# Last stage of a one-core transformer block: turning tiles by transposing transfers instead of on TensorE, and a new order of the engines' work

## What is computed

```python
h = layernorm(x) * (1 + ca) + sa
x = x + ga * attention(h)                  # 16 heads; the 409 queries of largest norm in each head
h = layernorm(x) * (1 + cb) + sb
gate = fp4_linear(h, w_gate); y = fp4_linear(h, w_up)      # 1408 columns each
x = x + gb * fp4_linear(silu(gate) * y, w_down)
# fp4_linear quantises both operands in blocks of 16: scale = max|block| / 6, values rounded to a grid of eight magnitudes
```

## Time and profile before

| | |
|---|---|
| median of 3 runs | 3645.56 us (3643.36 to 3648.74) |
| the profiled execution's own time | 3647.05 us |
| its span | 3645.2 us |
| TensorE's granted clock over the span | 0.957 of full speed |
| TensorE busy (matmul) | 3308.7 us, 91% |
| VectorE, GpSimd, ScalarE busy | 2764.1, 1512.2, 1035.5 us (76%, 41%, 28%) |
| DMA | 252.71 MB, mean 69 GB/s |

### The profile page before, as it was taken

How to read it: one execution, slowest core, us unless ns; L and a number is a source line. 1 busy time by engine, 2 the same in 40 slices (tenths; PEclk the granted TensorE clock), 3 DMA queues, 4 the chain that set the end, 5 groups by cost and what they waited for, 6 DMA issues and landing times. The chain is left out here.

```text
span 3645.2 us, 50953 instructions
## 1 busy us (share of the span) xinstructions
PE 3308.7 (91%) x16784; PEld 1498.4 (41%) x16784; DVE 2764.1 (76%) x3797; ACT 1035.5 (28%) x1454; POOL 1512.2 (41%) x1311
## 2 busy tenths in 40 slices
PE   5999997036999999999986999999999999999998
PEld 2554553021323332333323555555555555555554
DVE  4677675975666666666645898989898989898986
ACT  1332331003555555555541111111111111111111
POOL 0332331004555555555533444444444444445442
PEclk8999998567999999999997999999999999999999
DMA  5656556102222222222212100010101010101000
...
DMA packets 194398, 252.71 MB, mean 69 GB/s; under 512 B 58581, under 2 KB 114261, under 8 KB 193493
## 3 DMA queue, kind: packets, MB, share of 16 engines
...
## 5 line engine op out<-in xcount | busy, mean ns | idle before, releaser
L1038 DVE TENSOR_REDUCE top<-ps_max 128x1 f32<-128x1024 f32 (+1 forms) x512 | 618.5, 1219 | 340.9 <-PE ps_max L1171 340.8
L1117 ACT ACTIVATE p<-ps_exp,p_bias 128x820 f32<-128x820 f32 x512 | 483.0, 943 | 457.6 <-PE ps_exp L1197 457.6
L1208 PE MATMUL ps_out<-p,v_tok 128*33 128x410 f32 x2048 | 453.0, 521 | 0.0
L1007 POOL DMA_INDIRECT o_d<-o_rows,chosen x256 | 249.0, 973 | 446.6 <-DVE o_rows L1064 373.7
L1642 ACT ACTIVATE silu<-f_g 128x512 f32<-128x512 f32 (+1 forms) x192 | 107.8, 561 | 801.5 <-PE f_u L1711 801.5
L1171 PE MATMUL ps_max<-k_max,q_max 96*128 96x512 f16 (+1 forms) x1024 | 314.4, 389 | 1.1 <-DVE top L1038 0.8
L1197 PE MATMUL ps_exp<-q_exp,k_exp 98*128 98x410 f16 x1024 | 266.7, 342 | 44.7 <-ACT p L1117 44.7
L1711 PE MATMUL f_g<-gu,xT_lo 128*128 128x512 f16 (+1 forms) x768 | 278.3, 362 | 0.0
L1709 PE MATMUL f_g<-gu,xT_hi 128*128 128x512 f16 (+1 forms) x768 | 278.1, 362 | 0.0
L1710 PE MATMUL f_g<-gu,xT_hi 128*128 128x512 f16 (+1 forms) x768 | 278.1, 362 | 0.0
L1709 PE MATMUL f_u<-gu,xT_hi 128*128 128x512 f16 (+1 forms) x768 | 277.5, 361 | 0.0
(11 more groups left out here) (201 smaller groups left out, 6417.7 us busy)
## 6 DMA issues: line engine op xcount, KB each, us to landing
...
a_in<-o_d SPq DMA_DIRECT2D x64, 256.0 KB, 2.6
```

What stands on the lines that cost most here:

```text
L1007: pool.indirect_dma_start(o_rows, bass.IndirectOffsetOnAxis(ap=con["chosen"][0:n, t, h:h + 1], axis=0), o_rows_of[u][0:n, t, :], None).the ...
L1038: ve.tensor_reduce(top[0:rows_of(t), t, half:half + 1], ps_max[c % 2][0:rows_of(t), :, :].rearrange("p a n -> p (a n)"), AX.X, ALU.max, ne ...
L1117: act.activation(p32[k % PB][:, :, :], ps_exp[:, :, 0:NQ], ACT.Exp, bias=con["p_bias"][:, 0:1], scale=scale).then_inc(p_done, 1)
L1208: last = pe.matmul(ps_out[at:at + VCOLS, 0:NQ], v_tok[u][:, t, :], p32[k % PB][:, s, :], start=k == 0, stop=k == STEPS - 1)
```

## The change

All three turns (attention's rows, quantised `xq`, quantised hidden tile) leave TensorE. Each tile is split into high and low fp16 parts first, in SBUF and in its own layout: ScalarE reads `a_in`, `xq1` or `xq2` (`high_of_a`, `high_of_x`, `high_of_hidden`; the hidden tile in one instruction of 1408 columns), VectorE the same and the high part (`low_of_a`, `low_of_x`, `low_of_hidden`). Then SP issues two transposing transfers, of the high and of the low part (`turn_a`, `turn_x`, `turn_hidden`). The two PSUM banks that held turned tiles become third banks for gate and up. The second normalisation moves from VectorE to ScalarE (`normalise`, an Identity activation with scale 1/deviation and a shift, which GpSimd now works out as a third small step in `deviation`). `take_attention` multiplies by `ga` while it takes the product out; GpSimd adds `ga * bo`, worked out once, to `x` instead (`residual`). The front of a tile (attention's product, residual, moments, normalisation, modulation) is done two slots ahead of its gate and up instead of one, and the order in each engine's slot is new. The result of the down product is added and stored two slots behind the tile instead of three. A few semaphores are shared between stages, and seven slots are written out at the end instead of three.

```diff
-        ps_t = [m.ps(f"f_t{k}", [P, 512]) for k in range(2)]
-        ps_g = [m.ps(f"f_g{k}", [P, 512]) for k in range(2)]
-        ps_u = [m.ps(f"f_u{k}", [P, 512]) for k in range(2)]
+        ps_g = [m.ps(f"f_g{k}", [P, 512]) for k in range(3)]
+        ps_u = [m.ps(f"f_u{k}", [P, 512]) for k in range(3)]
...
+def turn_a(t):
+    if has(t, -1):
+        hold(sp, w_ready, t, sp_held)
+    hold(sp, a_low, t + 1, sp_held)
+    for src, dst in ((a_hi, aT_hi), (a_lo, aT_lo)):
+        sp.dma_start_transpose(dst[:, :, :], src[:, :]).then_inc(a_turned, 16)
+
+def turn_x(t, t4):
+    u = t4 % 2
+    if has(t, -2):
+        hold(sp, g_ready, (t - 1) * NG, sp_held)
+    hold(sp, x_low, t + 1, sp_held)
+    for src, dst in ((x_hi, xT_hi[u]), (x_lo, xT_lo[u])):
+        sp.dma_start_transpose(dst[:, :, :], src[:, :]).then_inc(x_turned, 16)
+
+def turn_hidden(t):
+    if has(t, -1):
+        hold(sp, d_ready, t, sp_held)
+    hold(sp, hid_low, t + 1, sp_held)
+    for src, dst in ((hid_hi, hT_hi), (hid_lo, hT_lo)):
+        sp.dma_start_transpose(dst[:, :, :], src[:, :]).then_inc(hid_turned, 16)
...
+def slot(t, t4, b2, b_z):
     if has(t, 3):
-        load_a(t + 3, t4 + 3)
-    if has(t, -3):
-        store(t - 3, t4 + 1)
+        load(t + 3, t4 + 3)
+    if has(t, 4):
+        load_a(t + 4, t4 + 4)
+    if has(t, 3):
+        turn_a(t + 3)
+    if has(t, 1):
+        turn_x(t + 1, t4 + 1)
+    if has(t, -2):
+        store(t - 2, t4 + 2)
+    if has(t, -1):
+        turn_hidden(t - 1)
...
+def low_of_a(t, t4):
+    ve.wait_ge(a_high, t + 1)
+    ve.scalar_tensor_tensor(out=a_lo[:, :], in0=a_in[t4 % 2][:, :], scalar=O_UP, in1=a_hi[:, :], op0=ALU.mult,
+                            op1=ALU.subtract).then_inc(a_low, 1)
 
 def low_of_x(t):
-    ve.wait_ge(t_hi, turn1_at(t) + 1)
-    ve.tensor_tensor(xT_lo[:, :, :], ps_t[0][:, :].rearrange("p (c n) -> p c n", n=P), xT_hi[:, :, :],
-                     ALU.subtract).then_inc(t_lo, 1)
-
-def low_of_a(t):
-    ve.wait_ge(a_hi, t + 1)
-    ve.scalar_tensor_tensor(out=aT_lo[:, :, :], in0=ps_w[:, :].rearrange("p (c n) -> p c n", n=P), scalar=O_UP,
-                            in1=aT_hi[:, :, :], op0=ALU.mult, op1=ALU.subtract).then_inc(a_lo, 1)
-
-def take_attention(t):
+    ve.wait_ge(x_high, t + 1)
+    ve.tensor_tensor(x_lo[:, :], xq1[:, :], x_hi[:, :], ALU.subtract).then_inc(x_low, 1)
+
+def low_of_hidden(t):
+    ve.wait_ge(hid_high, t + 1)
+    ve.scalar_tensor_tensor(out=hid_lo[:, :], in0=xq2[:, :], scalar=H_UP, in1=hid_hi[:, :], op0=ALU.mult,
+                            op1=ALU.subtract).then_inc(hid_low, 1)
+
+def take_attention(t, b):
     ve.wait_ge(w_ready, t + 1)
     need(ve, x2_done, t)
-    ve.scalar_tensor_tensor(out=y[:, :], in0=ps_w[:, :], scalar=1.0 / (W_UP * O_UP), in1=bo[:, :],
-                            op0=ALU.mult, op1=ALU.add).then_inc(y_done, 1)
+    ve.scalar_tensor_tensor(out=y[:, :], in0=ps_w[:, :], scalar=1.0 / (W_UP * O_UP), in1=vec["ga"][:, b, :],
+                            op0=ALU.mult, op1=ALU.mult).then_inc(y_done, 1)
...
-def normalise(t, t4):
-    ve.wait_ge(frs_done, t + 1)
-    ve.tensor_scalar(h[:, :], x2[t4 % 4][:, :], mv[:, 0:1], rstd[:, 0:1], ALU.subtract, ALU.mult)\
-      .then_inc(fxh_done, 1)
...
 def hidden(t, k):
     c0, n = F_COLS[k]
+    if k == 0:
+        need(ve, q2_step, t * QS - QS + 4)
     ve.wait_ge(silu_done, t * NG + k + 1)
-    ve.scalar_tensor_tensor(out=hid[:, c0:c0 + n], in0=ps_u[k % 2][:, 0:n], scalar=1.0 / F_UP,
-                            in1=s32[k % 2][:, 0:n], op0=ALU.mult, op1=ALU.mult).then_inc(hid_done, 1)
+    ve.scalar_tensor_tensor(out=hid[:, c0:c0 + n], in0=ps_u[k][:, 0:n], scalar=1.0 / F_UP,
+                            in1=s32[k][:, 0:n], op0=ALU.mult, op1=ALU.mult).then_inc(hid_done, 1)
...
-def slot(t, t4, b1, b2, b_z):
-    low_of_x(t)
-    if has(t, -2):
-        low_of_hidden(t - 2, 0)
+def slot(t, t4, b2, b_z):
+    hidden(t, 0)
+    if has(t, 3):
+        low_of_a(t + 3, t4 + 3)
     if has(t, 1):
-        take_attention(t + 1)
-    if has(t, -2):
-        low_of_hidden(t - 2, 1)
+        quantise_h(t + 1)
+    if has(t, 2):
+        take_attention(t + 2, b2)
     if has(t, -1):
         hidden_add(t - 1)
     if has(t, 1):
-        moments(t + 1, t4 + 1)
+        low_of_x(t + 1)
     if has(t, -1):
         hidden_take(t - 1)
-    if has(t, 1):
-        normalise(t + 1, t4 + 1)
-    hidden(t, 0)
     if has(t, -2):
-        low_of_hidden(t - 2, 2)
+        take_down(t - 2, b_z)
+    if has(t, 2):
+        moments(t + 2, t4 + 2)
     hidden(t, 1)
-    if has(t, 2):
-        low_of_a(t + 2)
-    if has(t, 1):
-        quantise_h(t + 1)
+    if has(t, -1):
+        low_of_hidden(t - 1)
     hidden(t, 2)
     hidden_units(t)
-    if has(t, -2):
-        take_down(t - 2, b_z)
...
 def residual(t, t4, b):
-    hold(pool, y_done, t + 1, pool_held)
-    pool.tensor_tensor(y[:, :], y[:, :], vec["ga"][:, b, :], ALU.mult).then_inc(ga_done, 1)
-    pool.wait_ge(ga_done, t + 1)
-    pool.wait_ge(fx_in[t4 % 2], in_turn(t, t4))
+    hold(pool, fx_in[t4 % 2], in_turn(t, t4), pool_held)
+    pool.tensor_tensor(xt[t4 % 2][:, :], xt[t4 % 2][:, :], ga_bo[:, b, :], ALU.add).then_inc(xg_done, 1)
+    hold(pool, xg_done, t + 1, pool_held)
+    pool.wait_ge(y_done, t + 1)
     need(pool, res_done, t - 3)
     pool.tensor_tensor(x2[t4 % 4][:, :], xt[t4 % 2][:, :], y[:, :], ALU.add).then_inc(x2_done, 1)
 
+def deviation(t):
+    hold(pool, fmv_done, t + 1, pool_held)
+    pool.tensor_scalar(rstd[:, :], mv[:, 1:2], EPS, None, ALU.add).then_inc(frs_done, 1)
+    pool.wait_ge(frs_done, t * 3 + 1)
+    pool.tensor_tensor(rstd[:, :], rstd[:, :], half[:, :], ALU.pow).then_inc(frs_done, 1)
+    hold(pool, frs_done, t * 3 + 2, pool_held)
+    pool.tensor_scalar(shift[:, :], mv[:, 0:1], rstd[:, 0:1], -1.0, ALU.mult, ALU.mult).then_inc(frs_done, 1)
...
-def slot(t, t4, b1, b2, b_z):
-    if has(t, -3):
-        result(t - 3, t4 + 1)
+def slot(t, t4, b2, b_z):
     if has(t, 1):
-        residual(t + 1, t4 + 1, b1)
-        modulate(t + 1, b1)
+        scale_h(t + 1)
     if has(t, -1):
         scale_hidden(t - 1)
-    if has(t, 1):
-        scale_h(t + 1)
+    if has(t, -2):
+        result(t - 2, t4 + 2)
+    if has(t, 2):
+        residual(t + 2, t4 + 2, b2)
+        deviation(t + 2)
+        modulate(t + 2, b2)
...
+def normalise(t, t4):
+    act.wait_ge(frs_done, t * 3 + 3)
+    act.activation(h[:, :], x2[t4 % 4][:, :], ACT.Identity, bias=shift[:, 0:1], scale=rstd[:, 0:1])\
+       .then_inc(fxh_done, 1)
...
+def slot(t, t4, b2, b_z):
+    if has(t, 3):
+        high_of_a(t + 3, t4 + 3)
     gate(t, 0)
-    if has(t, -2):
-        high_of_hidden(t - 2, 2)
+    if has(t, 1):
+        high_of_x(t + 1)
+    if has(t, -1):
+        high_of_hidden(t - 1)
     gate(t, 1)
     if has(t, 2):
-        high_of_a(t + 2)
+        normalise(t + 2, t4 + 2)
     gate(t, 2)
...
+def slot(t, t4, b2, b_z):
+    gate_up(t, t4, 0)
     if has(t, 2):
-        turn_a(t + 2, t4 + 2)
-    gate_up(t, 2)
+        attention_out(t + 2)
     if has(t, -2):
         down(t - 2)
+    gate_up(t, t4, 1)
+    gate_up(t, t4, 2)
```

More of the change, by code:

```diff
@@ L1286, in feed_forward @@
         xn1, mg1, xq1 = (m.sb(f"q1_{k}", [P, D], F32) for k in ("xn", "magic", "xq"))
-        xT_hi = m.sb("xT_hi", [P, KC, P], F16)
-        xT_lo = m.sb("xT_lo", [P, KC, P], F16)
-        s32 = [m.sb(f"silu{k}", [P, 512], F32) for k in range(2)]
+        x_hi = m.sb("x_hi", [P, D], F16)
+        x_lo = m.sb("x_lo", [P, D], F16)
+        xT_hi = [m.sb(f"xT_hi{u}", [P, KC, P], F16) for u in range(2)]
+        xT_lo = [m.sb(f"xT_lo{u}", [P, KC, P], F16) for u in range(2)]
+        s32 = [m.sb(f"silu{k}", [P, 512], F32) for k in range(NG)]
         hid = m.sb("hid", [P, FF], F32)
@@ L1343, in drive @@
             for t in range(5):
-                slot(t, t % 4, 0, 0, 0)
-            with eng.Fori(1, NT // 4 - 1) as g:
+                slot(t, t % 4, 0, 0)
+            with eng.Fori(1, NT // 4 - 2) as g:
                 per = TILES // 4
@@ L1348, in drive @@
                 for s in range(4):
-                    slot(g * 4 + s + 1, (s + 1) % 4, now if s < 2 else then, now if s < 1 else then, before if s < 1 else now)
-            for t in range(NT - 3, NT):
-                slot(t, t % 4, B - 1, B - 1, B - 1)
+                    slot(g * 4 + s + 1, (s + 1) % 4, now if s < 1 else then, before if s < 1 else now)
+            for t in range(NT - TAIL, NT):
+                slot(t, t % 4, B - 1, B - 1)
             last()
@@ L1656, in slot, with first @@
+                def first():
+                    high_of_a(0, 0)
+                    high_of_a(1, 1)
+                    normalise(0, 0)
+                    high_of_a(2, 2)
+                    high_of_x(0)
+                    normalise(1, 1)
+                def slot(t, t4, b2, b_z):
+                    if has(t, 3):
+                        high_of_a(t + 3, t4 + 3)
                     gate(t, 0)
-                    if has(t, -2):
```

(42 more changed lines are left out.)

201 lines of the change are left out of this document (79 added, 122 removed).

## The result

The changed kernel takes 3815.05 us (median of 4 runs, 3813.5 to 3816.5) against 3645.56 us: a ratio of 1.0464, 95% interval 1.0446 to 1.0482. It is slower by 169.5 us, against 158 forecast.

The account below looks back on a forecast made before the run. A circle of waits through VectorE, GpSimd and ScalarE was taken to bound the kernel: 16.57 + 6.7 + 2.54 + 1.17 = 27.0, with two meetings 28.5 us a slot; 2.47 more x 64 = 158 us, so 3804 us, range 3690 to 4100.

Parts of the forecast that it names:

- The circle: VectorE, GpSimd and ScalarE, each ending a slot with work its next slot needs: 28.5 us a slot, for 26.03 before.
- VectorE 16.57: VectorE from the last piece of `hidden` to the end of `hidden_take` in the next slot: 16.57 us.
- the meeting at L1370: VectorE's instruction on 1408 columns beside GpSimd's `scale_h`: 1.30 us instead of 0.88 alone, so + 0.4.
- GpSimd 6.7: GpSimd's `scale_hidden`, `result` and two additions of `residual`, up to VectorE's `moments` of the tile two ahead: 6.7 us.
- `moments` to the last piece: `moments` to the power's end and third small step 2.54, ScalarE's `normalise`, gate and hand-overs 1.17, meeting of VectorE and GpSimd 1.1.
- The meeting with `low_of_hidden`: `low_of_hidden` on VectorE, both inputs in SBUF, beside GpSimd's power step: the power step ends about 1.1 us late.
- `normalise` on ScalarE: ScalarE's normalisation, taken as a silu of 512 columns: 0.60 us, with the last `gate`, 0.49, queued behind it.
- The wait at BN_STATS: Sign on VectorE: it should wait 3 to 4 us a slot for GpSimd's `x`; under 1 us makes the forecast wrong.
- x: From the end of `low_of_hidden` to both transferred parts landed: taken as 7 us, bounding only over 12.5, or 11 at lower clock.
- SP's issue: SP issues nine transfers a slot for three, at a third of a microsecond each.
- The transfers as a bound: Hidden tile's transposing transfers set the slot: 32.5 us and 4060, or 37.5 us and 4380; chance 0.22.
- Rival 3: TensorE stays the bound at 24.0 us a slot if GpSimd's three additions do not delay `moments`: 3517 us, chance 0.11.

Follow-up runs that it names:

- the better order: The changed kernel's work reordered on GpSimd, ScalarE and VectorE, TensorE waiting 0.55 us a slot for a transfer SP issues last: 0.9799 of the kernel before, 3570.9 us.
- the first eight: The follow-up runs before the reordered kernels: seven variants of the changed kernel, and the kernel before with transposing transfers; ratios from 1.0228 to 1.1129.
- the gate: The changed kernel with the third gate piece ahead of the normalisation on ScalarE: 1.0304 of the kernel before, 58 us faster than the changed kernel.
- the normalisation: The changed kernel with the normalisation back on VectorE and GpSimd's third small step gone: 1.0371 of the kernel before, 34 us faster than the changed kernel.
- the two banks: The changed kernel with gate and up in two banks each instead of three: 1.1115 of the kernel before, 237 us slower than the changed kernel.
- the bias addition: The changed kernel without GpSimd's addition of `ga * bo` (1.0251 of the kernel before), or with it at the head of GpSimd's slot (1.0399).
- the old order: The kernel before, its order kept, attention rows and hidden tile turned by transfers: 1.0228 of the kernel before; with `low_of_hidden` moved behind `moments`, 1.0076.

## Why the prediction was right

**The circle: right, within 0.4 us in each term.** VectorE 16.57 + 0.4 for the meeting at L1370: measured 17.38 (L1370 took 1.37 us, for 1.30). Most of the 0.4 too little is `hidden_units`, 5.10 us to the next first piece for the 4.84 taken. GpSimd 6.7: 6.59. `moments` to the last piece 2.54 + 1.17 + 1.1 = 4.81: 4.59. Sum 28.5, measured 28.56 in this slot and 28.66 over 31. That it agrees to 0.1 or 0.2 is partly luck, as errors of + 0.4, - 0.1 and - 0.2 cancel.

**The meeting with `low_of_hidden`: right in kind, wrong in place.** The power step was said to be drawn out to 1.5 us. It took its 0.57, beside `low_of_hidden`. The third small step, L1600, was held in its place: 1.02 us against the 0.23 taken, ending at 2783.42, 0.13 after `low_of_hidden`. It cost 0.8 instead of 1.1. The rule of the Trainium skill, page "SBUF — State Buffer", section "Who interferes with whom", by which a VectorE instruction with two SBUF inputs and a GpSimd one that reads SBUF exclude each other, fits L1600 and not the power step, which started 0.03 us ahead of L1485 and ran beside it. Nor did the other low parts pay, L1476 and L1481, 0.68 us each here; but GpSimd had nothing under way beside them in this order, so they don't test the rule.

**`normalise` on ScalarE: undersized.** 0.60 was taken from a silu; its record is 0.81, and the gate behind it starts 0.72 after it:

```profile
2783.46 0.81 ACT L1664 ACTIVATE f_h<-x,f_shift,f_rstd 128x512 f32<-128x512 f32 x1 [5.47 <-POOL f_shift L1600]
2784.18 0.47 ACT L1676 ACTIVATE silu<-f_g 128x384 f32<-128x384 f32 x1
```

These 0.1 us stand against the 0.3 that the meeting cost less.

**The wait at BN_STATS: mis-sized.** "3 to 4 us a slot" was said and 6.07 measured. GpSimd's stretch is 6.6 and VectorE has only `take_down`, 0.6, to do in it; the figure contradicted the prediction's own sum.

**TensorE: right in kind.** 84% was said, 88% measured: the work was put at 24.0 us a slot at the full clock and showed as 25.1, at a mean granted clock of 0.95 in the stretch. It still had cover.

**The transfers: hidden, as said**, with x = 5.4 instead of 7. The Trainium skill, page "DMA: Bandwidth & Descriptors", section "Latency and other measured facts", gave an estimate of 2.8 us plus a fixed part for the pair; the trace has 5.2 from the first issue (2783.39) to the second landing, of which SP's issue of the first is 1.4, so 2.4 us would be the fixed part, which the prediction left without a figure. **SP's issue** was taken as a third of a microsecond. It is 1.2 us for 512 columns and 1.4 to 1.6 for 1408, some 9 us a slot for all nine. Here it had cover. In the better order it was what TensorE waited for.

**The rivals.** The transfers as a bound are refuted by one more of them costing nothing, TensorE as the bound by the 6 us at BN_STATS. Rival 3 is refuted for the written order, the only one it asked about; a new order of the same instructions does reach TensorE's bound. The expectations behind the prediction did worse than it: of the first eight, three missed the size by a third or more (the gate, the normalisation, the two banks), the one of three more transfers missed its range, and one had the wrong sign. In the gate, the normalisation, the bias addition, the banks and the old order, one term of the circle had been changed and the others left at their old neighbours.
